# A decoder layer on one core: the second quarter of a head group's cross attention value products moved one step later in TensorE's order

## What is computed

```python
x = x + self_attention(layernorm(x))
q = (layernorm(x) @ Wq + bq)      # 16 heads of 8, 256 rows in each batch
k, v = ctx @ Wk + bk, ctx @ Wv + bv      # 512 rows in each batch
scores = where(mask == 0, -inf, q @ k.T / sqrt(8))
x = x + (softmax(scores) @ v) @ Wo + bo
x = x + experts(layernorm(x)) + shared_expert(layernorm(x))
```

## Time and profile before

| | us |
|---|---|
| median of 3 runs | 204.69 |
| lowest and highest run | 204.68, 205.4 |
| the profiled execution, its own time | 204.75 |
| its span in the trace | 202.9 |
| TensorE busy | 191.8 |
| DVE busy | 156.5 |
| ACT busy | 137.6 |
| POOL busy | 96.7 |

### The profile page before, as it was taken

One profiled execution on the slowest core, in us unless ns is written; L12 is line 12 of the kernel. 1 busy time (PEld: TensorE's weight loads), 2 busy tenths in 40 slices (PEclk: granted clock), 3 DMA queues, 4 the chain that ended last, 5 costly groups with the idle time before them and its releaser, 6 DMA issues.

```text
span 202.9 us, 4609 instructions
## 1 busy us (share of the span) xinstructions
PE 191.8 (95%) x1626; PEld 151.3 (75%) x1626; DVE 156.5 (77%) x418; ACT 137.6 (68%) x318; POOL 96.7 (48%) x145
## 2 busy tenths in 40 slices
PE   7999999899999779988999999999989999999995
PEld 7788787767877566755575657576668799999994
DVE  2579999668768695779989999999973866458744
ACT  2499878679767767289989898987976232452220
POOL 7599217688467757707739992003300017500430
PEclk9999999999999999999999999999999999999999
DMA  6980407703552015689632400000000000000001
GB/s 173 384 208 3 155 2 227 243 2 54 74 74 37 2 39 115 73 102 117 94 88 83 76 2 0 5 0 3 0 0 3 5 0 0 3 0 13 3 1 38
DMA packets 13301, 12.69 MB, mean 63 GB/s; under 512 B 1072, under 2 KB 11312, under 8 KB 13280
## 3 DMA queue, kind: packets, MB, share of 16 engines
q1 hardware_dynamic: 12176, 11.15, 25.8%
q10 hardware_dynamic: 1008, 1.06, 1.6%
q0 software_dynamic: 96, 0.20, 0.7%
HBM read 10.96 MB, written 1.44 MB: 61 GB/s over the span
## 4 chain that ended last, share of the span: by engine, by line
PE 71%; DVE 14%; ACT 8%; issue 5%; POOL 1%; DVEq 0%; ACTq 0%; POOLq 0%
PE ps L990 13%; PE ps L949 10%; PE ps L1014 8%; PE ps L926 6%; PE ps L875 6%; PE ps L759 6%; PE ps L908 5%; ACT prob L635 4%; PE ps L891 4%; PE ps L847 3%; DVE q_t L1220 3%; PE ps L731 3%; DVE low L1210 3%; PE ps L772 3%; DVE prob_t L1283 2%
## 5 line engine op out<-in xcount | busy, mean ns | idle before, releaser
L1220 DVE CUSTOM_DVE_ANT_0 q_t<-ps,mask_add 128x512 f32<-128x512 f32 x64 | 41.4, 685 | 3.4 <-PE ps L908 2.1
L509 POOL TENSOR_TENSOR prob<-prob,rec 128x512 f32<-128x512 f32 x32 | 32.7, 1047 | 22.8 <-DVE rec L1279 22.8
L635 ACT ACTIVATE prob<-ps,low 128x256 f32<-128x256 f32 x64 | 29.5, 487 | 7.4 <-DVE low L1210 7.4
L669 ACT ACTIVATE q_t<-q_t,low 128x512 f32<-128x512 f32 x44 | 29.4, 718 | 4.3 <-DVE low L1220 4.1
L949 PEld LDWEIGHTS ps<-ident,q_t 128*128 128x128 f32 x176 | 19.5, 141 | 9.4 <-ACT q_t L669 3.2
L949 PE MATMUL ps<-ident,q_t 128*128 128x128 f32 x176 | 24.1, 277 | 2.4 <-ACT place_k L712 0.8
L548 POOL TENSOR_TENSOR place_k<-place_k 128x256 f32<-128x256 f32 x10 | 7.3, 733 | 38.7 <-DVE place_k L1245 38.7
L1210 DVE TENSOR_REDUCE low<-ps 128x2 f32<-128x512 f32 x32 | 20.4, 683 | 5.9 <-PE ps L847 5.8
L655 ACT ACTIVATE q_t<-ps 128x512 f32<-128x512 f32 x18 | 10.6, 599 | 21.0 <-PE ps L990 21.0
L1266 DVE TENSOR_TENSOR q_t<-q_t,ps 128x512 f32<-128x512 f32 x18 | 12.2, 684 | 11.4 <-PE ps L990 8.2
L875 PE MATMUL ps<-prob_t,v 128*64 128x256 f32 x128 | 17.3, 390 | 2.3 <-DVE prob_t L1283 2.0
(11 more groups left out here) (183 smaller groups left out, 471.9 us busy)
## 6 DMA issues: line engine op xcount, KB each, us to landing
k_stack<-k_dram SPq DMA_DIRECT2D x18, 128.0 KB
wg<-in_L_ffn_w_gate SPq DMA_DIRECT2D x1, 1024.0 KB, 5.4
wu<-in_L_ffn_w_up SPq DMA_DIRECT2D x1, 1024.0 KB, 7.9
q_stack<-q_dram SPq DMA_DIRECT2D x6, 144.0 KB
k_dram<-prob SPq DMA_DIRECT2D x1, 768.0 KB, 3.6
w_in<-in_L_attn_Wq ACTq DMA_DIRECT2D x2, 256.0 KB, 5.4
context<-in_ctx SPq DMA_DIRECT2D x1, 512.0 KB, 5.7
w_in<-in_L_attn_Wv SPq DMA_DIRECT2D x1, 512.0 KB, 7.4
```

What stands on the lines that cost most here:

```text
L509: nc.gpsimd.tensor_tensor(pr, pr, rec1[:, s % 2, r, :].unsqueeze(2).to_broadcast([P, C, S]), ALU.mult).then_inc(s_norm1, 1)
L635: e = nc.scalar.activation(prob1[:, s % 3, r, c * S:(c + 1) * S], ps[:, 2 * (s % 2) + r, c * S:(c + 1) * S], ACT.Exp, bias=low1[:, s % 2, ...
L669: nc.scalar.activation(prob2[n % 3][:, c, :], score2[n % 2][:, c, :], ACT.Exp, bias=low2[:, n % 2, c:c + 1], scale=-1.0).then_inc(s_exp2, 1)
L1220: nc.vector.tensor_tensor_reduce(out=score2[n % 2][:, c, :], in0=ps[:, 2 * (n % 2) + c, :], in1=mask_add[:, c, :], scale=1.0, scalar=3e38, ...
```

## The change

For groups 0 to 5, the second quarter's products move from step 4k + 7 to step 4k + 8.

```diff
 VALUES2 = {}
 for k in range(B * NG):
-    later = {B * NG - 2: (1, 1, 2, 2), B * NG - 1: (0, 0, 0, 0)}.get(k, (1, 1, 3, 3))
+    later = {B * NG - 2: (1, 1, 2, 2), B * NG - 1: (0, 0, 0, 0)}.get(k, (1, 2, 3, 3))
     for kc in range(KC):
         VALUES2.setdefault(HG * (k + 1) + LAG_T + later[kc], []).append((k, kc))
```

## The result

The changed kernel took 206.06 us (median of 11 runs, 205.23 to 206.45), the kernel before, on the same chips, 205.11 us (11 runs, 204.41 to 205.4). The ratio is 1.0047, with a 95% interval of 1.0030 to 1.0064: a loss of 0.6 to 1.3 us. The loss is clear of the measurement. Its middle value lies just inside the 0.5% within which the prediction called it no change; the interval reaches to both sides of that line. The profiled execution's span went from 202.9 to 203.8 us.

A forecast was written before the change was run, and what follows sets the result against it. A ring DVE, ACT, PE, DVE was taken to bound the period. Terms 0 + 0 + 0.15 + 0.30 = 0.45 us on 204.75 gave 205.20, less 0.06 for the median: 205.1 us, range 204.0 to 206.6.

The forecast's parts named there:

- no change by over 0.5%: Whole kernel: a time from 203.67 to 205.71 us, which a measurement can't tell from no change; chance 0.75.
- Price of one more run, 0.22 us: PE, each of groups 0 to 5: entering and leaving the additional run of products costs 0.22 us.
- The upper bound of 0.58: PE, ends of a run: the weight loads' whole idle time, 0.17 in front and 0.41 behind, 0.58 us.
- the slower rival: PE, turn of step 4k + 9: run ends cost up to 0.58 us a group, total 207.2 us; chance 0.17.
- Groups 2 and 3, "Cost: nothing": Turn of step 4k + 9: could start at 127.12, still ahead of 127.20, so the 0.22 us costs nothing.
- the 0.33 of the text: PE ahead of the turn of step 4k + 9, groups 2 and 3: room of 0.33 us each.
- the handover: Between engines, as from DVE's copy to PE's turn of step 21: a price of 0.15 us.
- Groups 0 and 1, "0, with 0.05 either way": Groups 0 and 1 together: step 8's earlier turn is lost again; 0 us, with 0.05 either way.
- The faster rival: Steps 8 and 24: turns coming 0.44 us earlier are kept, 0.78 us gained, 204.0 us; chance 0.14.
- Group 4, +0.15: Step 25: its turn comes 0.22 us late, DVE's copy waits until 136.88; loss 0.15 us.
- Group 5, +0.30: Steps 28 and 29: L797 waits for POOL's rows, the turn of step 29 is 0.45 late, 0.15 included.
- the 18 idle times: PE's weight loads, groups 0 to 5: 18 idle times at the ends of runs where there were 12.

The follow-up runs named there:

- (1, 3, 3, 3): Groups 0 to 5: one quarter in step 4k + 7, three in one run in 4k + 9, against the kernel before; ratio 1.0051.

## Why the prediction was right and wrong

The measured loss is 0.95 us by the medians and 0.86 in the stage, and the time of 206.06 us lies in the range (204.0 to 206.6); no change by over 0.5% was the likeliest case. But the forecast of +0.45 us was half of the loss, and that 1.0047 stays under 1.005 is luck. Of the 0.96 by which 206.06 is over the forecast of 205.1, 0.42 comes from the kernel before, which took 205.11 in these runs and 204.69 in those that the forecast started from.

- *Price of one more run, 0.22 us.* Confirmed: step 19, with one quarter, lasts 1.97, which is the 1.31 of a step without products and 0.66 more. The upper bound of 0.58 was not needed, and the slower rival, which rested on it, did not come. The traces show an idle time of the weight loads at both ends of every run, 0.17 and 0.41, together 0.58, and PE loses 0.22 by them. The Trainium skill, page "TensorEngine Tiling (Array Packing)", section "Key Properties", has the rule that a change of tiling mode drains TensorE; the trace agrees in that both ends have idle time, but that the idle time is this drain no run here shows.
- *Groups 2 and 3, "Cost: nothing".* This is the step that failed. The text let the turn of step 4k + 8 "start 0.44 earlier" and asked only if DVE and ACT could use that; it did not ask if the turn itself could. It needs the copies of the step before, the same rule that the text had just used for step 4k + 9. It could come 0.22 earlier and no more on DVE's account, and its second half 0.04 on ACT's. With that, the scores of step 21 start 4.78 us after DVE's copy of step 18 (127.36 - 122.58) where they started 4.17 after it: 0.61 late, not 0.22. The room takes 0.30, the turn of step 21 is shorter by 0.14 now that it waits for nobody, and 0.17 is left in each period. So the room was 0.44 in all, more than the 0.33 of the text, which had left out the handover behind ACT's copy. Of the 0.61, 0.22 is the additional run and 0.39 the freed time that was waited off. By these numbers each of the two alone would have been covered in groups 2 and 3, and only their sum was not; this is an estimate, since no run has just one of them at this place.
- *Groups 0 and 1, "0, with 0.05 either way".* DVE's copy of step 14 is 0.14 late (114.31 for 114.17), by the same step. That the 0.44 won in step 8 would be lost again by step 10 was right but for 0.07: the copy of step 10 starts at 106.04, before at 106.11. The faster rival fell there.
- *Group 4, +0.15.* Measured 0.63 - 0.46 = 0.17, by the mechanism named. *Group 5, +0.30.* Measured 0.86 - 0.63 = 0.23. L797 does wait for POOL, as the text said, but starts 0.06 after POOL's rows, not the 0.15 taken for the handover (the profile's times of POOL are rough). The two groups alone cost 0.39, where the text had 0.45.

So by the measurements the sum should have been 0.46 for groups 0 to 3 beside 0.40 for 4 and 5. The sign that the prediction gave for its being wrong, a period of groups 2 and 3 that is longer than 8.1, is the one that came: 8.28. Of its signs of being right, step 4k + 7 of 1.97, the wait that goes from step 24 to step 25 and the 18 idle times came. Step 4k + 8 lasts 2.35 and not 1.97, and the turn of step 21 starts 0.46 after DVE's copy (127.81, for a copy that ends at 127.35) and not 0.15.

The best version among the runs is the kernel before with the third quarter of groups 0 to 3 ahead of the turn of step 4k + 9: ratios 0.9982 and 0.9990, the second interval reaching 1.0002, so a gain of 0.1 to 0.2%. For groups 0 to 3 the runs show that each way tried to put the second quarter later costs something, and where; for group 4 the run with (1, 3, 3, 3) points the other way. Which order of all would be the best was not searched.

## What to carry to other kernels

When engines hand work around a ring with one buffer between them, time that is freed upstream is kept only as far as the next wait on that buffer: before calling a moved instruction covered by room further on, ask of every instruction between its old and its new place if it could really start earlier. The room that an instruction may fill is the idle time right ahead of the wait it stands in front of; an additional run of one quarter gained 0.32 us where it was the third quarter put there, and lost 0.47 where it was the second quarter put behind the turn of the step before. And two edits that use the same room don't add: together these two cost 1.61.

## What the runs showed that I had not expected

How little total work says here: the table with one run less in each group, and so 0.22 us less for PE in each, was 4.94 us slower in the stage. And how exactly the stage repeats: two profiled executions of the same kernel gave 62.05 both times, and the two halves of the change, run apart, add up to the whole, 0.47 + 0.39 = 0.86, while whole runs of the kernel before spread from 204.37 to 206.03 us.
